# Warm-up products between the first context transposes, and an earlier bias sum, in a cross-attention and quantised feed-forward kernel

## The reference

```
xn   = layernorm(x)                        # per row, eps 1e-5
s    = xn @ ctx.T / 0.72
a    = softmax(s) * mask                   # mask is 0 or 1.43
o    = a @ ctx + attn_bias
x1   = x + o @ weights
h    = layernorm(x1)
q    = clip(round(h / scale), -128, 127)   # scale = max(max|h|, 1e-6) / 127, per row
out  = x1 + (q @ weight_q.T) * scale * weight_scale + ffn_bias
```

## Time and profile before

| | us |
|---|---|
| median of 3 runs | 340.8 |
| range of the runs | 340.61 to 341.39 |
| profiled execution | 341.07 |
| its span, first to last instruction | 339.3 |

### The profile page before, as it was taken

How to read it: one execution, slowest core, us unless ns; L and a number is a source line. 1 busy time by engine, 2 the same in 40 slices (tenths; PEclk the granted TensorE clock), 3 DMA queues, 4 the chain that set the end, 5 groups by cost and what they waited for, 6 DMA issues and landing times.

```text
span 339.3 us, 6055 instructions
## 1 busy us (share of the span) xinstructions
PE 329.1 (97%) x1574; PEld 263.3 (78%) x1574; DVE 308.6 (91%) x630; ACT 226.8 (67%) x455; POOL 236.4 (70%) x368
## 2 busy tenths in 40 slices
PE   6999999999999999999999999999999999999992
PEld 6988777778777788877778887777888877787781
DVE  3697899999899999999999999999999999999887
ACT  4456676766667786666777767667776666777651
POOL 4175567778777777877777787877777877767642
PEclk9999999999999999999999999999999999999999
DMA  7939854445665544556654555565454556400002
GB/s 237 285 100 251 183 139 117 121 127 163 128 172 153 139 148 123 160 133 170 169 139 131 135 153 140 153 170 150 130 136 140 151 143 170 139 33 31 31 33 94
DMA packets 64545, 47.67 MB, mean 140 GB/s; under 512 B 20112, under 2 KB 51088, under 8 KB 64528
## 3 DMA queue, kind: packets, MB, share of 16 engines
q1 hardware_dynamic: 64528, 47.47, 51.9%
HBM read 35.13 MB, written 8.39 MB: 128 GB/s over the span
## 4 chain that ended last, share of the span: by engine, by line
PE 70%; DVE 9%; issue 1%; ACT 1%; DMA 1%; DVEq 0%; SPq 0%
PE ps_attn L515 7%; PE ps_scores L515 7%; PE ps_scores L517 7%; PE ps_scores L516 7%; PE ps_attn L517 7%; PE ps_attn L516 7%; PE ps_ffn L676 7%; PE ps_vw L515 6%; PE ps_vw L516 6%; PE ps_vw L517 6%; PE ps_pt L507 3%; DVE ffn_out L950 1%; DVE abs_max L963 1%; DMA xq_t<-x_int 1%; PE ps_xt L599 1%
## 5 line engine op out<-in xcount | busy, mean ns | idle before, releaser
L752 ACT ACTIVATE x_norm<-x_blocks,norm_spread 128x128 f32<-128x128 f32 x124 | 51.2, 483 | 2.3 <-ACT norm_spread L745 1.5
L1206 POOL TENSOR_TENSOR ct_lo<-ct_raw,ct_hi 128x512 fp32r<-128x512 f32 x28 | 36.3, 1298 | 23.0 <-ACT ct_hi L730 23.0
L515 PE MATMUL ps_attn<-vw_hi,pt_hi 128*128 128x512 f32 x124 | 51.4, 415 | 0.0
L515 PE MATMUL ps_vw<-w_hi,ct_hi 128*128 128x512 f32 x116 | 50.7, 437 | 0.0
L1159 POOL TENSOR_TENSOR scaled<-meanvar,scale 128x2 f32<-128x2 f32 x32 | 16.6, 517 | 46.6 <-DVE meanvar L913 46.6
L515 PE MATMUL ps_scores<-ct_hi,xt_hi 128*128 128x512 f32 x124 | 48.7, 393 | 0.0
L517 PE MATMUL ps_scores<-ct_hi,xt_lo 128*128 128x512 f32 x124 | 48.5, 391 | 0.0
L516 PE MATMUL ps_scores<-ct_lo,xt_hi 128*128 128x512 f32 x124 | 48.4, 391 | 0.0
L517 PE MATMUL ps_attn<-vw_hi,pt_lo 128*128 128x512 f32 x124 | 48.4, 390 | 0.0
L516 PE MATMUL ps_attn<-vw_lo,pt_hi 128*128 128x512 f32 x124 | 48.3, 389 | 0.0
L854 ACT ACTIVATE x_neg<-x,meanvar 128x512 f32<-128x512 f32 x31 | 22.5, 724 | 38.6 <-DVE meanvar L1122 38.6
(11 more groups left out here) (164 smaller groups left out, 779.5 us busy)
## 6 DMA issues: line engine op xcount, KB each, us to landing
x_in<-in_x_dram SPq DMA_DIRECT2D x32, 256.0 KB, 3.1
mask_in<-in_mask_BxSxS_fk_dram SPq DMA_DIRECT2D x32, 256.0 KB, 3.7
out_dram<-out_tile SPq DMA_DIRECT2D x31, 256.0 KB, 2.2
x_blocks<-in_x_dram SPq DMA_DIRECT2D x60, 128.0 KB, 3.6
ctx_in<-in_ctx_dram SPq DMA_DIRECT2D x56, 128.0 KB, 2.8
ctx_in<-in_ctx_dram SPq DMA_DIRECT2D x4, 256.0 KB, 4.6
x_blocks<-in_L_xattn_weights_dram SPq DMA_DIRECT2D x4, 256.0 KB, 6.5
xq_t<-x_int SPq DMA_TRANSPOSE x26, 2.4
```

What stands on the lines that cost most here:

```text
L515: nc.tensor.matmul(bank_, lhs_hi(t), rhs_hi(t), start=(t == 0), stop=False)
L752: last = nc.scalar.activation(x_norm[:, k, a * P:(a + 1) * P], x_blocks[:, slot(n, 4), a * P:(a + 1) * P], ACT.Identity, bias=norm1_spread ...
L1206: nc.gpsimd.tensor_tensor(ct_lo[:, batch_of(n), :, j * P:(j + 1) * P], ct_raw[:, slot(n, 2), :, :], ct_hi[:, batch_of(n), :, j * P:(j + 1) ...
```

## The change

Behind the transposes of context tiles 0 and 1, TensorE runs two more warm-up products into `ps_ffn` each (tiles 2 and 3 have none behind them). SP issues the load of the bias column behind the weights and ahead of x tile 1, before its wait for the turned context tiles, instead of behind x tile 2. VectorE takes the statistics of x tile 2 behind the four instructions of `bias_terms` instead of ahead of them.

```diff
--- before.py
+++ after.py
@@ -68,6 +68,8 @@
 FILLS = 8
 
 WARM_UPS = 7
+
+BETWEEN = 2
 
 LAST_WARM_UPS = 8
 
@@ -401,15 +403,15 @@
             for t in range(NT):
                 sp.dma_start(w_raw[:, t, :], weights.rearrange("(p t) e -> p t e", t=NT)[:, t, :]) \
                     .then_inc(w_loaded[t], 16)
+            with nc.allow_non_contiguous_dma(reason="512 bias values, one per partition and chunk"):
+                sp.dma_start(attn_bias_col[:, :], attn_bias.rearrange("(p t) -> p t", t=NT)) \
+                    .then_inc(attn_bias_loaded, 16)
             load_x(1 * P, 1)
 
             sp.wait_ge(first_ct_done, 2)
             load_blocks(ctx_in, ctx_flat, PER_BATCH * P, PER_BATCH, 2, ctx_loaded)
             load_mask(0, 0)
             load_x(2 * P, 2)
-            with nc.allow_non_contiguous_dma(reason="512 bias values, one per partition and chunk"):
-                sp.dma_start(attn_bias_col[:, :], attn_bias.rearrange("(p t) -> p t", t=NT)) \
-                    .then_inc(attn_bias_loaded, 16)
             sp.dma_start(wq_words[:, :, :], weight_q.rearrange("(t p) i -> p t i", p=P)).then_inc(wq_loaded, 16)
             load_x(3 * P, 3)
             load_mask(1 * P, 1)
@@ -573,6 +575,8 @@
                                                ctx_in[:, t, :].rearrange("p (c t) -> p t c", t=NT)[:, i, :],
                                                identity[:, :])
                 last.then_inc(first_ct_done, 1)
+                if t < PER_BATCH - 2:
+                    warm_up(ps_ffn, BETWEEN)
 
             def step(base, d):
                 if is_tile(base, d, 0):
@@ -926,9 +930,8 @@
             for i in range(NT):
                 dve.wait_ge(w_hi_ready, i + 1)
                 lo_part(w_lo[:, i, :], w_raw[:, i, :], w_hi[:, i, :], w_lo_ready)
-            for t in range(1, 3):
-                x_statistics(HEAD, PER_BATCH + t)
-                x_mean_var(PER_BATCH + t)
+            x_statistics(HEAD, PER_BATCH + 1)
+            x_mean_var(PER_BATCH + 1)
             dve.wait_ge(attn_bias_loaded, 16)
             nc.vector.tensor_scalar(bias_terms[:, :], w_raw[:, 0, :], attn_bias_col[:, 0:1], None,
                                     ALU.mult).then_inc(bias_terms_ready, 1)
@@ -937,6 +940,8 @@
                 nc.vector.scalar_tensor_tensor(out=bias_terms[:, :], in0=w_raw[:, t, :],
                                                scalar=attn_bias_col[:, t:t + 1], in1=bias_terms[:, :], op0=ALU.mult,
                                                op1=ALU.add).then_inc(bias_terms_ready, 1)
+            x_statistics(HEAD, PER_BATCH + 2)
+            x_mean_var(PER_BATCH + 2)
 
             def step(base, d):
                 def scale_ffn(n):
```

## The result

The changed kernel takes 337.82 us (median of 4 runs, 337.53 to 338.03) against 340.83 for the one before; the ratio of the two is 0.9915, with a 95% interval of 0.9894 to 0.9935. It is faster by 3.0 us, outside the forecast range (338.4 to 341.2) on the fast side. Its profiled execution took 337.69 us with a span of 335.9, 3.4 us less than that of before.

The account below looks back on a forecast made before the run. TensorE was taken to bind the first 33 us, VectorE the pace from there to 86.57. VectorE's 1.77 plus 0.48 of slack gave 2.25 off the profiled 341.07: 338.8, taken as 338.9, range 338.4 to 341.2.

Parts of the forecast that it names:

- TensorE binds in the first 33 us, and VectorE has 0.48 us in hand: Up to tile 1's `neg_max` at 33.27, TensorE sets the pace; VectorE waits 0.48 us there for its scores.
- By itself part two is worth nothing, because TensorE binds at 33.27: Bias column and VectorE order alone: 0.82 us gained on VectorE is lost waiting for TensorE's scores at tile 1's `neg_max`.
- part two: Earlier bias column load and bias terms ahead of tile 2's statistics: takes 0.82 us of idle time off VectorE.
- Part one: Warm-up products added between context transposes: fill TensorE's 1.34 us gap, raise its clock sooner, TensorE gains 2.5 us.
- My 7.0 us for the rise: TensorE's high clock comes 6.0 us after 1.00, counting the 0.23 us gap as nothing; before, it came at 13.9.
- VectorE's term: VectorE from the `ct_raw` transpose on: 0.82 us of idle time removed, 1.77 earlier with the warm-up part.
- 2.5 forecast for TensorE: TensorE's six score passes at the high clock end at 12.4 instead of 14.99 us.
- the slack: VectorE's 0.48 us wait for TensorE at tile 1's `neg_max`, added to its 1.77 for 2.25 us.
- The rise doesn't move: Rival: transposes may not raise TensorE's clock, only score products do; rise at 14.15, time 341.2 us, chance 0.18.
- The costs at nothing: Delays of SP's context loads and of GpSimd's tile 2 factors were expected to add no time.
- SP's later issues: SP's loads behind the second turned context tile go out 0.9 us later, costed at nothing.
- GpSimd's factors: Tile 2's factors on GpSimd near 20.4 us or later, `ct_lo` near 20.5: costed at nothing, 0.4 us without cover.

Follow-up runs that it names:

- b_again: The kernel before, unchanged, run and profiled a second time: 340.67 us, ratio 0.9999.
- warm_only: The kernel before with the four added warm-up products alone, bias column and statistics left in place: 341.19 us, ratio 1.0.
- bias_only: The kernel after without the four added warm-up products, keeping the bias column's earlier load and VectorE's new order: 338.70 us, ratio 0.9935 to before.
- a_again: The kernel after, unchanged, run and profiled a second time: 338.41 us, ratio 0.9927 to before.
- bias_5: The kernel after without the four added warm-up products, measured again with more runs: 338.74 us, ratio 0.9931 to before.
- after_5: The kernel after, unchanged, measured again with more runs: 338.32 us, ratio 0.9916 to before.
- turned_start_b: The kernel after without the four added products, fourteen transposes of ones replacing the seven starting warm-ups, second profile: 338.20 us, ratio 0.9934 to before.
- turned_start: The kernel after without the four added products, fourteen transposes of ones replacing the seven starting warm-ups: 338.60 us, ratio 0.9925 to before.
- bias_no_warm: The kernel after without any warm-up products, neither the seven at the start nor the four added: 339.05 us, ratio 0.9939 to before.

## Why the prediction was wrong

- **The direction** was right, the size (2.2 us forecast from the profiled execution, 3.0 between the medians) and the range were not.
- **What bounds the kernel.** "TensorE binds in the first 33 us, and VectorE has 0.48 us in hand" was true of the one execution shown; in none of the 17 other profiles does `neg_max` of tile 1 wait for TensorE. Its clock rose at 13.9 us; in the 14 other profiles with warm-ups or transposes at the start it was up at about 8 us or sooner. That execution took 341.07 us and `b_again`, with the early rise, 340.35: the early clock alone is worth little, because x tile 2 lands when it does, and the wait of 0.82 us for it in the earlier trace rows only grows. I read the spread of 340.61 to 341.39 as the play of the clock. Landings play at least as much: `warm_only` and `b_again`, both with an early rise, were profiled at 341.77 and 340.35, with x tile 2 landing 1.3 us apart. What spread the unprofiled runs isn't shown.
- **"By itself part two is worth nothing, because TensorE binds at 33.27" is the step that failed.** It is worth 2.1 us by `bias_only` (where `a_again` gains 2.4) and 2.7 by `bias_5` (where `after_5` gains 3.1), nearly the whole gain, and needs both its halves. The wait that it removes is 2.13 us in `b_again`, not 0.82: with an early clock VectorE comes to tile 2's statistics at 14.2 and not at 15.6.
- **Part one, the forecast's main step,** is worth nothing alone (`warm_only` 1.0 [0.9975, 1.0025]) and nothing measurable with part two. The high clock is there without it. My 7.0 us for the rise rested on the 6.0 us of work without a gap ahead of the one rise that I had seen; with the same seven products first it came at 4.8 in `b_again`.
- **VectorE's term** was 1.77 at the context turn and is 2.82 between the two profiles: `w_lo` was done 2.14 earlier instead of 0.95, the rest, 0.68, is most of the removed wait of 0.82. `w_lo` could not have come much sooner: ScalarE's copy of the last weight chunk, which it needs, waited for the chunk's load, and this limits what an early clock gives the changed kernel:

```profile
11.33 0.63 ACT L785 ACTIVATE w_hi<-x_blocks 128x512 fp32r<-128x512 f32 x1 [0.54 <-DMA x_blocks<-in_L_xattn_weights_dram]
```

  I had held the start of tile 2's transposes to the 7.88 of the earlier trace rows. That tile was there by 6.26 in the profile after: its landing varies. TensorE's first `ps_vw` product came at 11.10, 3.89 earlier against the 2.5 forecast for TensorE. How `neg_max` adds the slack to it (0.48 forecast, 0.57 found) and how the shift runs unchanged to the end were right. That the forecast came as near as 2.2 against 3.0 is in part luck: I gave part one what any early clock would give an execution whose own came late, and most executions of the kernel before have the early clock already, if the profiles speak for them.
- **The rivals.** "The rise doesn't move" was right that, behind the seven products, the added ones aren't needed for it, and wrong that the time then stays. Its rule, from the Trainium skill's "TensorE: Matmul & The Clock Gate", section "Part 4: PE-mode transpose", that the full clock doesn't engage in transpose mode, doesn't hold for this kernel's `nc.tensor.transpose`, whose mode the trace doesn't show: in `turned_start_b` a group of four transposes takes 0.93 us, 6.26 to 7.19, and from 7.80 on 0.48, with no other product before them.
- **The costs at nothing.** SP's later issues didn't come about: the loads behind the second turned tile went out at 6.01 in the profile after, against 6.58 in the first of before and 7.30 in `b_again`, where that tile landed late. GpSimd's factors were, as costed, under cover: `ct_lo` began at 19.04.

## What to carry to other kernels

One profile of a start is one draw of the clock and of every landing; before a chain is built on it, ask what each engine would wait for next if the odd thing (here a rise at 13.9 us) were not there. A wait of 0.8 us on a DMA can be a wait of 2 us that something else has shortened. And where two loads land within 0.5 us of each other and feed the same engine, as x tile 2 and the bias column do here, an experiment that moves one of them alone can show nothing (ratios of 0.998 to 1.001) though both together give nearly the whole gain.

## What was not expected of the hardware

Of the same code, the second context tile was turned at 5.49 in one profile of before and at 6.52 in the other, behind a wait of 1.33 us for its load, and the third at 7.88 and 7.21: landings of the first loads differ by one microsecond and more. x tile 2, issued at 9.65 and 9.70 in `b_again` and `warm_only`, landed at 16.35 and 17.68 by VectorE's start behind it. It was late together with what stood ahead of it: the last block of the context loads, issued at 8.66 and 8.70, took 6.2 and 7.8 us to land. Transposes alone bring TensorE from 1.2 to 2.4 GHz, as warm-up products do (`turned_start`, `turned_start_b` and, at some 9.3 us, `bias_no_warm`). The granted clock column reads 1.00 over the low-clock start of every profile; only the pitch of the products shows the rise.
